# Back turns of a routing stage: ordinary fp32 products in the place of transposes

## What is computed

```python
theta = relu(mean(gcn_conv(layernorm(x)), axis=0)) @ W2 + b2
coefs = (2 * sigmoid(theta) - 1).reshape(C, 4) * lambdas + init_v
x = x + max(xn[:, :, None] * coefs[None, :, :2] + coefs[None, :, 2:], axis=-1)   # xn = layernorm(x)

h = layernorm(x)                                                 # 6250 rows of 256
topk_vals, topk_idx = top_k(h @ gate_w + gate_b, 2)
moe = sum over the two chosen experts e of softmax(topk_vals) * (relu(h @ w1[e] + b1[e]) @ w2[e] + b2[e])
x = x + layernorm(h + moe) * gamma + beta
```

## Time and profile before

| | |
|---|---|
| Time, median of 3 runs | 893.68 us (891.11 to 896.88) |
| Span of the profiled execution | 882.4 us |
| TensorE busy (matmul) | 741.0 us, 84% |
| VectorE busy | 676.2 us, 77% |
| ScalarE busy | 475.4 us, 54% |
| GpSimd busy | 282.7 us, 32% |
| Chain that ended last, by engine | TensorE 60%, VectorE 23%, issue 8%, DMA 3%, ScalarE 3% |

### The profile page before, as it was taken

The page is one execution under the profiler, slowest core; times in us unless marked ns, Lnnn a source line. Parts: engine busy times, 40 slices in busy tenths (PEclk is TensorE's granted clock), DMA queues, the critical chain, the costliest instruction groups (busy, mean ns, idle before and its releaser), DMA issues.

```text
span 882.4 us, 21305 instructions
## 1 busy us (share of the span) xinstructions
PE 741.0 (84%) x6322; PEld 643.2 (73%) x6322; DVE 676.2 (77%) x1837; ACT 475.4 (54%) x1199; POOL 282.7 (32%) x313
## 2 busy tenths in 40 slices
PE   3555788888885776897899999999999999998893
PEld 3555355555555765876889999999998999997682
DVE  6999699999963688776757777777776777775597
ACT  5995677777635675653334444444444444443253
POOL 8400000000000457777734544544422222223010
PEclk9999699999997676568999999999999999999796
DMA  9850444445616944459999999899999999893999
GB/s 270 223 162 1 130 148 152 165 142 175 172 64 237 227 133 145 128 152 292 254 278 280 267 264 263 266 264 261 269 254 335 323 260 273 262 262 116 353 319 200
DMA packets 156240, 192.82 MB, mean 219 GB/s; under 512 B 78235, under 2 KB 125262, under 8 KB 153036
## 3 DMA queue, kind: packets, MB, share of 16 engines
q1 hardware_dynamic: 127048, 109.40, 44.7%
q10 hardware_dynamic: 15448, 51.04, 17.4%
q0 software_dynamic: 13632, 31.03, 11.2%
HBM read 151.05 MB, written 40.34 MB: 217 GB/s over the span
## 4 chain that ended last, share of the span: by engine, by line
PE 60%; DVE 23%; issue 8%; DMA 3%; ACT 3%; SPq 2%; DVEq 0%; ACTq 0%; POOL 0%; POOLq 0%
PE PS L1296 21%; PE PS L1308 19%; DVE W L1357 8%; PE PS L1334 4%; DVE W L1388 3%; DVE W L1423 3%; PE PS L1090 3%; PE PS L1186 2%; PE PS L1201 2%; DMA R<-xs 2%; PE PS L1214 2%; PE PS L1110 2%; SPq L719 2%; PE PS L1054 1%; DVE st L1464 1%
## 5 line engine op out<-in xcount | busy, mean ns | idle before, releaser
L1296 PEld LDWEIGHTS PS<-R,W 128*128 128x128 f32 x1808 | 223.1, 195 | 17.2 <-DVE R L1640 11.9
L1296 PE MATMUL PS<-R,W 128*128 128x128 f32 x1808 | 225.1, 278 | 9.7 <-DVE R L1640 9.7
L992 ACT ACTIVATE R<-PS,b1T 128x128 f32<-128x128 f32 x350 | 102.9, 367 | 233.9 <-PE PS L1296 233.8
L1308 PE MATMUL PS<-W,R 128*128 x904 | 213.9, 380 | 0.0
L610 POOL DMA_INDIRECT ys<-W,R x113 | 109.7, 971 | 230.9 <-DVE W L1692 228.5
L1308 PEld LDWEIGHTS PS<-W,R 128*128 128x128 f32 x904 | 163.6, 191 | 17.4
L1357 DVE TENSOR_TENSOR W<-R,W 128x3136 bf16<-128x3136 bf16 (+1 forms) x104 | 157.2, 1571 | 0.7 <-PE PS L1070 0.7
L890 ACT ACTIVATE W<-PS 128x1024 f16<-128x1024 f32 x104 | 106.2, 1023 | 38.0 <-PE PS L1090 32.0
L603 POOL DMA_INDIRECT xs<-W,slot_i x98 | 101.8, 1039 | 75.0 <-DVE slot_i L1522 46.3
L1090 PE MATMUL PS<-W,table 114*128 114x512 f16 x208 | 66.3, 403 | 26.3 <-DVE W L1388 25.9
L595 POOL MEMSET R<- 128x261 f32 x1 | 0.3, 317 | 226.4 <-PEq L1132 226.4
(11 more groups left out here) (264 smaller groups left out, 1028.9 us busy)
## 6 DMA issues: line engine op xcount, KB each, us to landing
W<-in_L_ffn_w ACTq DMA_DIRECT2D x96, 512.0 KB, 5.0
W<-key_rows SPq DMA_DIRECT2D x26, 784.0 KB
W<-in_L_ffn_w SPq DMA_DIRECT2D x33, 512.0 KB, 8.5
R<-xs SPq DMA_DIRECT2D x113, 130.5 KB
W<-ys SPq DMA_DIRECT2D x4, 2048.0 KB, 13.0
R<-xs SPq DMA_DIRECT2D x224, 32.0 KB
XH<-in_x SPq DMA_DIRECT2D x6, 896.0 KB, 11.7
W<-xs SPq DMA_DIRECT2D x116, 32.0 KB
```

Of the source, the lines that this page charges most:

```text
L992: last = act.activation(HT3[:, u, j, :], up_out(u, j), ACT.Relu, bias=b1T[:, ds(e, 1), j])
L1296: last = nc.tensor.matmul(up_out(u, j), W1S[b][:, k, j * P:(j + 1) * P], XT3[:, u, k, :], start=(k == 0), stop=(k == 1))
L1308: last = nc.tensor.matmul(PS[:, 6 * u, 0:C], HT3[:, u, j, :], wt2(e * W2COLS, j), start=(j == 0), stop=(j == 3))
```

## The change

The turns of back(q) are ordinary matrix products. The block of bra that is to be turned is the stationary operand, as it is for a transpose, and the identity is the moving operand; the result, in the same place of TB, is the block's transpose times the identity. Each product starts and ends its own accumulation. Nothing else changes: the waits, the signal behind the last product, the order of the instructions on every engine, the buffers. The line after is numbered one higher in the changed kernel, and so are all that follow.

```diff
                     for j in range(n):
                         for k in range(2):
-                            last = nc.tensor.transpose(TB[:, j, k * P:(k + 1) * P], bra[q % 2][:, k, j, :], ident[:, :])
+                            last = nc.tensor.matmul(TB[:, j, k * P:(k + 1) * P], bra[q % 2][:, k, j, :], ident[:, :],
+                                                    start=True, stop=True)
                     last.then_inc(returned, 1)
```

## The result

The changed kernel takes 900.73 us (median of 5 runs, 899.99 to 911.89), the kernel before 891.11 us beside it: 1.0132 of before, 95% interval 1.0088 to 1.0176, or 9.6 us more. Ratios and intervals leave out executions more than 1.5% above the fastest of the same kernel; medians are of all runs. The changed kernel was run once more beside the experiments: 903.46 us against 891.62, 1.0154 (1.0099 to 1.0209), 11.8 us. The forecast was 10.0 us more, and 903.7 us: most of the 3.0 us between that and 900.73 is the kernel before, which took 893.68 us in the runs that the forecast started from.

What follows compares the result with a forecast made beforehand. Expert stage bound by a never-resting TensorE, routing ahead of it by a ring of three engines with TensorE often at half clock; 17.1 us added less 7.1 given back, +10.0 on 893.7, makes 903.7 us; range 896 to 910 us.

Steps and rivals of the forecast that it cites:

- Price of a record: Back turns, line 1186: 0.213 us per record at half clock, 0.111 at full; 196 records replace 98.
- The sum on the chain: Routing stage: added records cost 18.4 us at the clock of before, 1.3 hidden, so 17.1 us reach the chain.
- the ring: Routing stage, about 276 to 398 us: TensorE, VectorE and ScalarE hand each other small pieces; no engine is full.
- 18.4 us by the forecast: Back turns: 74 added records at half clock (15.8 us) and 24 at full (2.7 us), before hiding.
- The cover of 1.3 us: Blocks at 308.19 and 336.36 us: growth of 0.67 us each, hidden by TensorE's wait for ScalarE's normalising.
- What the clock gives back: Second half of routing: longer unbroken streams bring full clock for a third of 54.61 us, returning 7.1 us.
- The first half: Routing stage, 282.38 to 336.99 us: full clock for 44% of it before, a share the forecast left unchanged.
- the 17.1 us of the sum: Routing stage: cost of the added records at the clock of before, 18.4 us less 1.3 hidden.
- 33 points from nothing: Routing from 336.99 to 391.60 us: share of full clock taken to rise from 0 to a third.
- The passing on: Routing's delay reaches the end: GpSimd's scatters, with 13 us of room, neither soften it nor add to it.
- The 11.3 us "around the span": Median of 893.68 us less the profiled span of 882.4 us, taken to lie around the span, untouched.
- 892.4 us: Whole kernel: the forecast span of the profiled execution after the change, beside a forecast time of 903.7 us.

Runs made afterwards that it cites:

- transposes twice: Kernel before with each back turn issued twice as a transpose, the second over the first: 904.67 us against 889.06, 1.017.
- with zeros: Kernel before plus four products of zeros in TensorE's wait ahead of the back turns of each group's first chunk: 884.64 us, 0.9948 of before.
- the half-changed kernels: Kernel before with ordinary products only in the first seven chunks, 896.51 us against 891.62 (1.0043), or only in the last eight, 899.48 us (1.0103).
- the changed kernel with the same zeros: Changed kernel plus four products of zeros ahead of the back turns of each group's first chunk: 896.36 us, 1.0067 of before.

## Why the prediction was right

**Price of a record.** Forecast 0.213 and 0.111 us, measured 0.212 and 0.116; two records for a product, as L1296 had shown. Right.

**The sum on the chain.** Right in kind: the additions sit in the ring. The last add of x ended in the changed kernel's first profile at 397.11 + 0.96 = 398.07 us, 120.6 us behind the first back turn; in that of before it ended at 385.32 + 0.96 = 386.28 us, 110.4 us behind (its row stands below). That is +10.1 us (120.55 less 110.42), the forecast to the tenth, in one pair of executions, and luck: in the second profiles the same add ended 107.80 and 123.52 us behind the first back turn (275.33 and 274.35 us), +15.7. The mean is 12.9 us; the whole stage to the first expert tile grew by 13.4 us, and the times by 9.6 and 11.8. The first expert tile starts at 411.57 and 409.99 us, where the forecast had it near 408. The added records, 18.4 us by the forecast at the clock of before, took 17.9 on line 1186. VectorE's rows, the kernel before twice and the second profile of the changed one:

```profile
385.32 0.96 DVE L1461 TENSOR_TENSOR XH<-PS,W 128x768 f32<-128x768 f32 x1 [2.02 <-PE PS L1186]
...
382.17 0.96 DVE L1461 TENSOR_TENSOR XH<-PS,W 128x768 f32<-128x768 f32 x1 [2.03 <-PE PS L1186]
...
396.91 0.96 DVE L1462 TENSOR_TENSOR XH<-PS,W 128x768 f32<-128x768 f32 x1 [0.67 <-PE PS L1186]
```

The cover of 1.3 us shrank at one place (the wait behind the block at 315.87 us is 0.52 us, where the earlier trace rows have 2.24) and was overrun at the other, since that block ran at half clock. At the first place the second profiles have 1.25 us before and 1.71 after, so the wait changes between executions by more than the 0.67 us it was to hide. The first profile of the changed kernel:

```profile
315.87 1.61 PE L1186 MATMUL PS<-ident,R 128*128 128x128 f32 x12 [1.92 <-DVE R L1453]
318.00 0.63 PE L1202 MATMUL PS<-ident,W 128*128 128x128 f32 x4 [0.52 <-ACT W L950]
...
345.50 2.92 PE L1186 MATMUL PS<-ident,R 128*128 128x128 f32 x12 [2.56 <-DVE R L1453]
348.21 0.97 PE L1202 MATMUL PS<-ident,W 128*128 128x128 f32 x4
```

**What the clock gives back.** The step was right in kind, and the experiments with transposes twice and with zeros show it: longer streams of either kind raise the share of full clock, and full clock shortens the stage. More TensorE work always went with the longer streams, and the runs don't separate the two. The first half kept its share, as I had let it (0.68 and 0.73, then 0.73 and 0.62), and the give-back on TensorE fell into the second part, as I had placed it; the times of the half-changed kernels don't show that. In size it was a guess that came near. I had taken 7.1 us; the two profiles of each kernel give 4.6 us of time, and the 17.1 us of the sum less the measured 11.8 or 9.6 give 5.3 or 7.5. I had let the share rise by 33 points from nothing, in a stretch that by chance had none in that execution; it rose by 14 to 34 points in the whole second part. Not all of what TensorE saves can be had. Its other work took 8.6 us less and the stage got about half of that. In the changed kernel TensorE went through its gates at full clock and then waited 7.25 us at a place where the kernel before waited 4.78 us. In the second profile of before the clock was full at those gates, without the change, and the wait was 6.96 us. TensorE's timeline there, first of the kernel before, twice, then of the changed one (the bracket is the idle time ahead of the block):

```profile
351.58 1.94 PE L1186 MATMUL PS<-ident,W 128*128 128x128 f32 x8 [4.78 <-issue]
...
350.23 1.94 PE L1186 MATMUL PS<-ident,W 128*128 128x128 f32 x8 [6.96 <-issue]
```

```profile
352.88 0.44 PE L1202 MATMUL PS<-ident,W 128*128 128x128 f32 x2
360.57 3.75 PE L1186 MATMUL PS<-ident,W 128*128 128x128 f32 x16 [7.25 <-issue]
```

There VectorE builds the list of the first 13 expert tiles ahead of the add of x that this block waits for (the add ends at 360.47 us, the block starts at 360.57); what TensorE wins before that place is lost in the wait.

**The passing on.** Right: the scatters had still more room. The last one and the load of the fourteenth expert tile, in the changed kernel, 20 us apart (13.5 in the earlier trace rows):

```profile
445.90 1.55 POOL L603 DMA_INDIRECT xs<-W,slot_i  x1 [0.30 <-issue]
...
465.55 1.85 SPq L719 DMA_DIRECT2D R<-xs  x4
```

The chain of the changed kernel reads otherwise at one point: it goes through GpSimd's scatters from 376.59 to 398.1 us. The row in which it turns there, and VectorE's row of the last add of x:

```profile
397.01 1.09 DMA xs<-W,slot_i
398.21 0.73 SPq L318
```

```profile
397.11 0.96 DVE L1462 TENSOR_TENSOR XH<-PS,W 128x768 f32<-128x768 f32 x1 [3.20 <-PE PS L1186]
```

SyncE's queue waits for several signals there, the last add of x among them. A scatter's landing and the add ended within 0.03 us of each other, and the chain took the landing, one of the group that starts at 376.59 us, which this wait doesn't need. In the second profile of the changed kernel the chain has no scatter in this stage and goes through the back turns.

**What was wrong.** The 11.3 us "around the span" do not lie around it. The changed kernel's first profiled execution took 911.89 us for a span of 910.2 us, the second one of before 886.99 us for 885.2 us: 1.7 and 1.8 us. So the first page of before was probably that of an execution of some 884 us, a fast one, and the gap to the median was the spread of executions. It did no harm since only the difference was added to the median; had I compared the span after with 892.4 us, it would have misled by 18 us.

## What to carry to other kernels

An fp32 transpose by the identity and an fp32 product by the identity differ on TensorE by the number of records, one against two, and by nothing else that these runs show; where TensorE's blocks sit in a ring with other engines, as here, that number is paid, less what full clock gives back. When a change lengthens TensorE's streams in a stage at half clock, put a second term beside the price: what full clock would give the rest of the stage, bounded by the waits for the other engines. One profile of each kernel is not enough where the clock falls differently from execution to execution: compare stages over two profiles, and times over many runs.

## What I had not expected of the hardware

The same kernel spreads widely: the kernel before took 882.63 to 901.37 us in 23 runs beside the first experiments, and the longer an execution, the lower its mean granted clock (correlation -0.76 over these runs, -0.82 over the 17 beside the later ones). With the zeros in the waits it took 882.14 to 888.28 us in 12 runs, a third of that spread, but the changed kernel with the same zeros took 889.61 to 902.58 in 12. So the zeros don't steady the time as such. The runs show the spread and that it goes with the clock, not where it comes from.
